# Maxima scores of latent and context attention taken for four head pairs in a row, with new order tables

## The chip, the cores and the metric

The kernel runs on one core of one Trainium2 chip. The metric is the device time of one execution in microseconds (us). TensorE is called PE, VectorE DVE, ScalarE ACT, GpSimd POOL and SyncE SP, as in the profile.

## What is computed

Two layers of a pre-norm decoder run over 32 sequences of 256 tokens with 256 features. Six steps follow each other for every sequence, and each adds its result to x:

```python
x = x + latent_attention(layernorm(x))            # 16 heads of 16, keys and values through a latent of 64
x = x + head_attention(layernorm(x), ctx)         # per token, 16 heads of 64 attend to each other; ctx 256 x 256
x = x + mixture_of_depths(layernorm(x))           # half of the tokens go through a 256-1024-256 network
x = x + sparse_attention(layernorm(x))            # of each score row only the 25 largest keep their value
x = x + context_attention(layernorm(x), ctx, len) # 16 heads of 16, keys from len on are masked
x = x + ternary_linear(layernorm(x))
```

## The kernel before

Everything is float32 but for a few bf16 helpers. The six steps are cut into four streams. Stream m is latent attention. Stream h is head attention and, at its end, mixture of depths (MoD). Stream t is sparse attention. Stream c is context attention and the ternary linear step. The streams work on different sequences at the same time: in one lap, m has the newest sequence, h the one before, t the next older and c the oldest. A lap is one sequence's worth of work on each stream. The steady part of the program holds 28 laps.

Every stream is a Python generator for each engine, and each `yield` in it ends a chunk. `woven` draws the chunks of the four streams in the order that a table gives. `ORDER["pe"]`, `ORDER["act"]`, `ORDER["dve"]` and `ORDER["pool"]` are strings of the letters m, h, t and c, one letter for each chunk. They cover four laps and are repeated seven times; `ORDER_FIRST` and `ORDER_LAST` are the laps before and after. An engine runs its instructions strictly in that order, so a chunk that waits for a semaphore holds up all chunks behind it. `FILL` says at which chunks, and how often, `fill` (L423) adds a matmul without use to PE's queue.

Streams m and c share the buffers `bufM` and the four PSUM banks `bankM`, and so follow one another. Their attention is `tensor_at` on PE. The 16 heads are 8 pairs; with 2 halves of the queries this makes 16 units. The keys of a pair (2 heads of 16 rows) lie in one strip of 32 partitions, and there are four such strips in each half `e` of `kT` and `q2`. First come the maxima: eight chunks of two units each, a pair in one of the strip couples (0, 1) and (2, 3), in `at_scores` (L494; the mask is added by the matmul of L489 in stream c). Each unit fills one bank, and DVE reduces it to the row maximum in `scores_max` (L504). Two chunks with their four units fill the four banks. Then POOL splits the maxima in three bf16 parts (L513), `shift_rows` (L528) and `shift_copy` bring them into rows, and `at_scores_T` (L550, L553) makes the scores transposed, two units to a chunk, in three banks. `exps_T` (L567) takes the exponential, and `at_values_T` (L580) multiplies with the values into `bankM[2]`. `at_out_pe1`, `at_out_dve` and `at_out_pe2` (L630, L639, L643, L652) divide by the sums.

Stream t scores a head pair in `at_scores` in its own banks `bankT`, ACT copies the scores to `sc` (L1019), and DVE finds the 25 largest of each row with four rounds of MAX8 (L1068) and MATCH_REPLACE8 (L1072) over two halves. POOL then makes the exponents from `wk` and `sc` (L1093, L1096, L1102, L1105), ACT takes the exponential (L1029), PE transposes (L595), ACT copies (L604), and PE multiplies with the values (L615). The heads are numbered r0 to r15 below. Stream t of a sequence begins only when MoD of the same sequence has added its update (L947), and when its own lap before has ended with the add of L688; then come layer norm (L427 to L461), projections (L467, L475) and the first scores. Selection of the next lap cannot begin before that.

MoD at the end of stream h is this on PE: the score row, then the chunk `sel` (L793, L797), which waits for ACT's pick matrix (L879), which waits for DVE's ranks (L930, L934); then the first layer in two chunks (L808), Gelu on ACT (L890), the second layer in eight (L814, L815) and the chunk `u` (L820).

## Time and profile before

| What | Value |
|---|---|
| median of three runs | 5935.59 us (5928.25 to 5955.03) |
| the profiled execution | 5922.4 us, of which the span is 5920.6 us |
| PE busy | 5310.9 us, 90% of the span |
| DVE busy | 4492.6 us, 76% |
| ACT busy | 3746.6 us, 63% |
| POOL busy | 2304.2 us, 39% |
| granted TensorE clock, mean | 0.95 of full speed |

Busy time counts a stretch once, however many instructions overlap in it. Matmuls in different strips of the array overlap, and so do consecutive ones with their tails; what a run of matmuls costs is read from the start of the run to the start of the next. A float32 matmul stands as two records. DVE's instructions overlap by their fixed part as well.

### The profile page before, as it was taken

To read this page: it belongs to the slowest core of one execution; us is meant where nothing else is said; L and a number is where in the kernel's file an instruction comes from. 1 tells how busy PE (TensorE), PEld (TensorE's weight loads), DVE (VectorE), ACT (ScalarE), POOL (GpSimd) and SP (SyncE) were. 2 spreads that over 40 slices of the span, in tenths; PEclk is the share of its full clock that TensorE was granted. 3 is DMA by queue.
4 is the path that set the end of the run, shared out by engine and by line. 5 is a ranking of instruction groups with operands and counts; after the bars stand their busy time and mean duration, and the time that the engine had idled before them with its cause. 6 is when DMAs were issued, how large, how long until landed. Compare 5 with 4: busy or idle time off the path is not lost.

```text
span 5920.6 us, 113246 instructions
## 1 busy us (share of the span) xinstructions
PE 5310.9 (90%) x39450; PEld 3769.4 (64%) x39450; DVE 4492.6 (76%) x16125; ACT 3746.6 (63%) x9377; POOL 2304.2 (39%) x4100
## 2 busy tenths in 40 slices
PE   7899989999989989989899989999989999989987
PEld 4666666666667666666666666666666666666654
DVE  2577787777787777887777787777787777788684
ACT  3566666666676666666666676666666666666642
POOL 0244443334443433443334443334443334443341
PEclk7899999999999999999999999999999999999876
DMA  2000000000000000000000000000000000000000
GB/s 90 6 5 7 7 8 8 5 8 7 7 8 8 5 8 5 9 8 8 5 8 7 7 9 8 5 8 7 7 8 8 5 8 7 7 8 8 1 4 6
DMA packets 29342, 52.98 MB, mean 9 GB/s; under 512 B 8145, under 2 KB 9810, under 8 KB 27986
## 3 DMA queue, kind: packets, MB, share of 16 engines
q1 hardware_dynamic: 28770, 45.73, 2.5%
q8 instruction: 313, 5.13, 0.4%
q14 instruction: 259, 2.12, 0.1%
HBM read 37.33 MB, written 8.39 MB: 8 GB/s over the span
## 4 chain that ended last, share of the span: by engine, by line
PE 42%; DVE 36%; ACT 14%; issue 4%; POOL 2%; ACTq 0%; DVEq 0%; POOLq 0%
DVE wk L1072 13%; DVE m L1068 9%; PE bankH L737 8%; PE bankM L494 4%; DVE m_nm L504 4%; DVE m_last L1068 3%; ACT xk_area L835 3%; PE bankM L467 3%; PE bankH L760 2%; ACT xq_area L835 2%; PE bankH L808 2%; PE bankH L814 2%; PE bankT L475 2%; PE bankT L467 2%; PE bankM L475 2%
## 5 line engine op out<-in xcount | busy, mean ns | idle before, releaser
L1072 DVE MATCH_REPLACE8 wk<-m,wk 128x256 f32<-128x256 f32 x2048 | 822.5, 409 | 0.0
L1093 POOL TENSOR_SCALAR mx<-m 128x2 f32<-128x2 f32 x512 | 114.3, 223 | 1737.7 <-DVE wk L1072 1732.4
L504 DVE TENSOR_REDUCE m_nm<-bankM 128x2 f32<-128x512 f32 x1024 | 651.8, 682 | 148.3 <-PE bankM L494 146.0
L1068 DVE MAX8 m<-wk 128x8 f32<-128x256 f32 x2048 | 759.9, 413 | 0.0
L1102 POOL TENSOR_TENSOR t_pr<-wk,sc 128x256 f32<-128x256 f32 x1024 | 739.2, 742 | 2.5 <-PE bankT L595 1.3
L1105 POOL TENSOR_TENSOR t_pr<-t_pr,sc 128x256 f32<-128x256 f32 x1024 | 729.4, 733 | 0.0
L835 ACT ACTIVATE xk_area<-bankH,xb 64x256 f32<-64x256 f32 x1024 | 479.7, 468 | 244.2 <-PE bankH L737 225.5
L1029 ACT ACTIVATE t_pr<-t_pr,t_nm 128x256 f32<-128x256 f32 x1024 | 476.5, 510 | 155.9 <-POOL t_pr L1105 143.1
L553 PE MATMUL bankM<-m_q,m_kT 32*128 32x512 f32 x2048 | 552.7, 619 | 0.0
L494 PE MATMUL bankM<-m_kT,m_q 32*128 32x256 f32 x4096 | 526.2, 393 | 10.1 <-DVE m_nm L504 8.9
L595 PE MATMUL bankT<-ident,t_pr 128*128 128x128 f32 x2048 | 339.2, 290 | 124.6 <-ACT t_pr L1029 122.1
L494 PEld LDWEIGHTS bankM<-m_kT,m_q 32*128 32x128 f32 x4096 | 376.3, 191 | 80.2 <-issue 23.4
L604 ACT ACTIVATE t_pt<-bankT 128x512 f32<-128x512 f32 x512 | 308.4, 602 | 175.5 <-PE bankT L595 171.1
L1072 DVE MATCH_REPLACE8 wk<-m_last,wk 128x256 f32<-128x256 f32 x1024 | 411.4, 409 | 0.0
L1072 DVE MATCH_REPLACE8 wk<-m,sc 128x256 f32<-128x256 f32 x1024 | 411.3, 409 | 0.0
L1068 DVE MAX8 m<-sc 128x8 f32<-128x256 f32 x1024 | 379.8, 413 | 29.5 <-ACT sc L1019 28.2
L595 PEld LDWEIGHTS bankT<-ident,t_pr 128*128 128x128 f32 x2048 | 236.7, 145 | 258.7 <-ACT t_pr L1029 209.0
L567 ACT ACTIVATE m_pT<-bankM,keymask 128x512 f32<-128x512 f32 x512 | 338.0, 692 | 96.4 <-PE bankM L553 93.5
L1019 ACT ACTIVATE sc<-bankT 128x512 f32<-128x512 f32 x512 | 306.4, 602 | 119.6 <-PE bankT L494 116.6
L1068 DVE MAX8 m_last<-wk 128x8 f32<-128x256 f32 x1024 | 379.7, 413 | 0.0
L580 PE MATMUL bankM<-m_pT,m_va 128*32 128x256 f32 x4096 | 355.4, 427 | 18.0 <-ACT m_ot L587 14.5
L567 ACT ACTIVATE m_pT<-bankM 128x512 f32<-128x512 f32 x512 | 282.6, 594 | 106.6 <-PE bankM L553 104.5
(224 smaller groups left out, 11691.4 us busy)
## 6 DMA issues: line engine op xcount, KB each, us to landing
xin<-x_in SPq DMA_DIRECT2D x32, 256.0 KB, 2.6
ctxA<-ctx_in SPq DMA_DIRECT2D x32, 256.0 KB, 2.6
ctxB<-ctx_in SPq DMA_DIRECT2D x32, 256.0 KB, 2.6
out<-x SPq DMA_DIRECT2D x32, 256.0 KB, 2.0
w<-w_w SPq DMA_DIRECT2D x2, 1024.0 KB
xwq<-w_xwq SPq DMA_DIRECT2D x1, 1024.0 KB
xwk<-w_xwk SPq DMA_DIRECT2D x1, 1024.0 KB
xwv<-w_xwv SPq DMA_DIRECT2D x1, 1024.0 KB
```

Source lines behind the costliest of these rows:

```text
L494: last = nc.tensor.matmul(bank[x][:, j * S:(j + 1) * S], b["q2"][r:r + 32, e, j, t * P:(t + 1) * P], b["kT"][r:r + 32, e, :], start=not ma ...
L504: nc.vector.tensor_reduce(b["nm"][:, i % 2, 2 * (i // 2) + x, :], banks[u % 4][:].rearrange("p (j s) -> p j s", j=2), AX.X, ALU.max, negat ...
L553: nc.tensor.matmul(bank[x][:], b["kT"][r:r + 32, e, c * P:(c + 1) * P], b["q2"][r:r + 32, e].rearrange("p j s -> p (j s)"), start=False, s ...
L567: nc.scalar.activation(b["pT"][c][:, x, :], bank[(0, 1, 3)[(2 * i + x) % 3]][:], ACT.Exp, bias=0.0 if bias is None else bias[:, c:c + 1]). ...
L595: last = nc.tensor.transpose(bank[:, (2 * c + j) * P:(2 * c + j + 1) * P], b["pr"][:, u % 2, j, c * P:(c + 1) * P], w["ident"][:])
L737: last = nc.tensor.matmul(bank[:, hp * S:(hp + 1) * S], w[wt][:, d, c:c + P], src[:, d, :], start=(d == 0), stop=(d == ND - 1))
L835: nc.scalar.activation(dst[0:XD, :, 8 * h:8 * h + 8].rearrange("p (j a) u -> p j a u", a=2), bankH[1 - TURNS.index("vqk"[which] + str(quad ...
L1029: nc.scalar.activation(b["pr"][:, u % 2, t, :], sp_[:, u % 2, t, :], ACT.Exp, bias=b["nm"][:, u, t:t + 1], scale=-1.0 / BIG).then_inc(g["s ...
L1068: link.inc(nc.vector.max(top, src[:, t, :]))
L1072: m = nc.vector.match_replace(out=wk[:, k, t, :], in_to_replace=take, in_values=src[:, t, :], imm_value=-BIG)
L1102: nc.gpsimd.tensor_tensor(taken[:, u % 2, t, :], wk[:, u % 2, t, :], sc[:, u % 3, t, :], ALU.subtract).then_inc(g["sp_tk"], 1)
L1105: nc.gpsimd.tensor_tensor(sp_[:, u % 2, t, :], taken[:, u % 2, t, :], sc[:, u % 3, t, :], ALU.mult).then_inc(g["sp_mul"], 1)
```

## The change

For the maxima, `pair_scores` takes four units at once, one in each strip and each with a bank of its own (`SIDE = 4`): eight chunks of an attention become four. A group waits until DVE has reduced all four units of the group before. Units are renumbered: four strips first, then the half of the queries, then `e`. The transposed scores keep two units to a chunk (`DEEP = 2`), but in the new numbering a chunk of strips 0 and 1 is followed by one of strips 2 and 3; the values take the heads and the PSUM halves accordingly. The order of operations of a unit, the waits on semaphores between engines and all instructions of ACT, DVE and POOL keep their kind and number. The order tables of all four engines are new, and so are the numbers of fills: 53 in four laps before, 91 after. In the new tables of PE the chunks of MoD from `sel` to `u` stand farther ahead in stream t. Before, `sel` stood behind the transpose of r14 and `u` at the end of the same lap of stream t. Now `sel` stands behind the transpose of r11, and `u` behind that of r13 in three laps of four and of r15 in one. On DVE, the ranks stand behind the end of r11 or within r12, where they stood behind r15.

The core of the diff (the strings of the order tables are left out):

```diff
...
+SIDE, DEEP = 4, 2
...
-FILL = {"t": ["00020100", "02010111", "00020101", "02010011"],
-        "h": ["20111000100", "00211000000", "00121000100", "01111100000"],
-        "c": ["00", "12", "21", "12"],
-        "m": ["110", "010", "110", "010"]}
...
+FILL = {"t": ["00002000", "00012121", "22021003", "02132010"],
+        "h": ["01213100000", "13010010000", "11103112130", "02012102022"],
+        "c": ["10", "00", "20", "03"],
+        "m": ["110", "023", "110", "233"]}
...
-CHUNKS = {"pe": dict(h=57, t=39, c=34, m=33),
+CHUNKS = {"pe": dict(h=57, t=39, c=30, m=29),
...
         def strip(pr):
             return pr // 4, 32 * (pr % 4)
 
-        def at_scores(n, b, bank, i, masked=False):
+        def at_scores(n, b, bank, i):
 
             m, t = i // 2, i % 2
-            for x in range(2):
-                if masked:
-                    r = strip(2 * m + x)[1]
-                    nc.tensor.matmul(bank[x][:], mask_lhs[r:r + 32, :], mrow[r:r + 32].rearrange("p t s -> p (t s)"), start=True, stop=False,
-                                     skip_group_check=True)
             for j in range(2):
                 for x in range(2):
                     e, r = strip(2 * m + x)
                     last = nc.tensor.matmul(bank[x][:, j * S:(j + 1) * S], b["q2"][r:r + 32, e, j, t * P:(t + 1) * P],
+                                            b["kT"][r:r + 32, e, :], start=True, stop=True)
+                    if j == 1:
+                        last.then_inc(g[n + "_s"], 1)
+
+        def pair_scores(n, b, units, masked):
+
+            if masked:
+                for u in units:
+                    r = 32 * (u % 4)
+                    nc.tensor.matmul(bankM[u % 4][:], mask_lhs[r:r + 32, :], mrow[r:r + 32].rearrange("p t s -> p (t s)"), start=True, stop=False,
+                                     skip_group_check=True)
+            for j in range(2):
+                for u in units:
+                    e, t, k = u // 8, u // 4 % 2, u % 4
+                    r = 32 * k
+                    last = nc.tensor.matmul(bankM[k][:, j * S:(j + 1) * S], b["q2"][r:r + 32, e, j, t * P:(t + 1) * P],
                                             b["kT"][r:r + 32, e, :], start=not masked, stop=True, skip_group_check=masked)
                     if j == 1:
                         last.then_inc(g[n + "_s"], 1)
 
-        def scores_max(dve, n, b, banks, u):
-
+        def scores_max(dve, n, b, u):
+
+            e, t, k = u // 8, u // 4 % 2, u % 4
             yield
             dve.wait_ge(*at(g[n + "_s"], u + 1))
-            i, x = u // 2, u % 2
-            nc.vector.tensor_reduce(b["nm"][:, i % 2, 2 * (i // 2) + x, :], banks[u % 4][:].rearrange("p (j s) -> p j s", j=2),
+            nc.vector.tensor_reduce(b["nm"][:, t, 4 * e + k, :], bankM[k][:].rearrange("p (j s) -> p j s", j=2),
                                     AX.X, ALU.max, negate=True).then_inc(g[n + "_nm"], 1)
 
         def shift_split(pool, n, b):
...
             act.wait_ge(*at(g[n + "_m3p"], 1))
             nc.scalar.activation(b["m3"][:], bank[:], ACT.Copy).then_inc(g[n + "_m3"], 1)
 
-        def at_scores_T(pe, n, b, bank, i):
-
-            m, c = i // 2, i % 2
-            bank = [bank[(0, 1, 3)[(2 * i + x) % 3]] for x in range(2)]
-            yield
-            if i == 0:
+        def pair_scores_T(pe, n, b, units):
+
+            bank = lambda v: bankM[(0, 1, 3)[v % 3]]
+            if units[0] == 0:
                 pe.wait_ge(*at(g[n + "_m3"], 1))
-            elif i >= 2:
-                pe.wait_ge(*at(g[n + "_ex"], 2 * i - 1))
-            else:
-                pe.wait_ge(*at(g[n + "_ex"], 1))
-            for x in range(2):
-                r = strip(2 * m + x)[1]
-                nc.tensor.matmul(bank[x][:], sel_b[r:r + 32, 2 * m + x, :], b["m3"][r:r + 32, :], start=True, stop=False, skip_group_check=True)
-            for x in range(2):
-                e, r = strip(2 * m + x)
-                nc.tensor.matmul(bank[x][:], b["kT"][r:r + 32, e, c * P:(c + 1) * P],
+            if units[-1] >= 3:
+                pe.wait_ge(*at(g[n + "_ex"], units[-1] - 2))
+            for v in units:
+                e, k = v // 8, v % 4
+                r = 32 * k
+                nc.tensor.matmul(bank(v)[:], sel_b[r:r + 32, 4 * e + k, :], b["m3"][r:r + 32, :], start=True, stop=False, skip_group_check=True)
+            for v in units:
+                e, c, k = v // 8, v // 4 % 2, v % 4
+                r = 32 * k
+                nc.tensor.matmul(bank(v)[:], b["kT"][r:r + 32, e, c * P:(c + 1) * P],
                                  b["q2"][r:r + 32, e].rearrange("p j s -> p (j s)"), start=False, stop=True,
                                  skip_group_check=True).then_inc(g[n + "_st"], 1)
 
-        def exps_T(act, n, b, bank, i, bias=None):
-
-            c = i % 2
+        def exps_T(act, n, b, i, bias=None):
+
+            c = i // 2 % 2
             for x in range(2):
                 yield
                 act.wait_ge(*at(g[n + "_st"], 2 * i + x + 1))
...
                     act.wait_ge(*at(g[n + "_pv"], i - 1))
                 if i == 0 and bias is not None:
                     act.wait_ge(*at(g["mask_row"], 2))
-                nc.scalar.activation(b["pT"][c][:, x, :], bank[(0, 1, 3)[(2 * i + x) % 3]][:], ACT.Exp,
+                nc.scalar.activation(b["pT"][i % 2][:, x, :], bankM[(0, 1, 3)[(2 * i + x) % 3]][:], ACT.Exp,
                                      bias=0.0 if bias is None else bias[:, c:c + 1]).then_inc(g[n + "_ex"], 1)
 
         def at_values_T(pe, n, b, bank, i):
 
-            m, c = i // 2, i % 2
+            e, c, y = i // 4, i // 2 % 2, i % 2
             yield
             pe.wait_ge(*at(g[n + "_ex"], 2 * i + 2))
             if i == 4:
                 pe.wait_ge(*at(g[n + "_ot"], 1))
+            if i % 4 == 0:
+                fill("c" if n == "crs" else "m", i // 4 + (n == "mla"), bank[:, S:S + P])
             for x in range(2):
                 for j in range(2):
                     r = 32 * (2 * x + j)
-                    last = nc.tensor.matmul(bank[r:r + 32, S * (m % 2):S * (m % 2 + 1)], b["va"][:, c, 4 * m + 2 * x + j, :],
-                                            b["pT"][c][:, x, S * j:S * (j + 1)], start=(c == 0), stop=(c == 1))
+                    last = nc.tensor.matmul(bank[r:r + 32, S * y:S * (y + 1)], b["va"][:, c, 8 * e + 4 * y + 2 * x + j, :],
+                                            b["pT"][i % 2][:, x, S * j:S * (j + 1)], start=(i % 4 == 0), stop=(c == 1), skip_group_check=True)
             last.then_inc(g[n + "_pv"], 1)
 
         def at_copy_ot(act, n, b, bank, half):
...
 
         def tensor_at(pe, n, masked):
             b = bufM
-            for i in range(8):
-                yield
-                if i == 0:
+            for u in range(0, 2 * PAIRS, SIDE):
+                yield
+                if u == 0:
                     pe.wait_ge(*at(g[n + "_kT"], 1))
                     pe.wait_ge(*at(g[n + "_qT"], 2))
                     pe.wait_ge(*at(g[n + "_va"], 1))
                     if masked:
                         pe.wait_ge(*at(g["mask_row"], 1))
-                elif i == 1 and masked:
-                    past(pe, "mla_x")
-                elif i == 1 and here("c"):
-                    pe.wait_ge(*at(g["lin_o"], 1))
-                elif i >= 2:
-                    pe.wait_ge(*at(g[n + "_nm"], 2 * i - 2))
-                at_scores(n, b, [bankM[2 * i % 4], bankM[(2 * i + 1) % 4]], i, masked)
+                if u <= 2 < u + SIDE:
+                    if masked:
+                        past(pe, "mla_x")
+                    elif here("c"):
+                        pe.wait_ge(*at(g["lin_o"], 1))
+                if u >= 4:
+                    pe.wait_ge(*at(g[n + "_nm"], u - 4 + SIDE))
+                pair_scores(n, b, range(u, u + SIDE), masked)
             yield from shift_rows(pe, n, b, bankM[2])
-            for i in range(9):
-                if i < 8:
-                    yield from at_scores_T(pe, n, b, bankM, i)
-                if i >= 1:
-                    yield from at_values_T(pe, n, b, bankM[2], i - 1)
-                if i in (2, 6):
-                    fill("c" if masked else "m", i // 4 + (not masked), bankM[2][:, S:S + P])
+            done = 0
+            for v in range(0, 2 * PAIRS, DEEP):
+                yield
+                pair_scores_T(pe, n, b, range(v, min(v + DEEP, 2 * PAIRS)))
+                while 2 * done + 2 <= v:
+                    yield from at_values_T(pe, n, b, bankM[2], done)
+                    done += 1
+            while done < PAIRS:
+                yield from at_values_T(pe, n, b, bankM[2], done)
+                done += 1
             yield from at_out_pe1(pe, n, b, [bankM[3], bankM[2]], 2)
             yield from at_out_pe2(pe, n, b, bankM[2])
 
...
             b = bufM
             yield from shift_copy(act, n, b, bankM[2])
             for i in range(8):
-                yield from exps_T(act, n, b, bankM, i, bias)
+                yield from exps_T(act, n, b, i, bias)
                 if i == 5:
                     yield from at_copy_ot(act, n, b, bankM[2], 0)
             yield from at_copy_ot(act, n, b, bankM[2], 1)
...
 
         def vector_at(dve, n):
             for u in range(2 * PAIRS):
-                yield from scores_max(dve, n, bufM, bankM, u)
+                yield from scores_max(dve, n, bufM, u)
             yield from at_out_dve(dve, n, bufM, [bankM[3], bankM[2]])
...
```

## Rows read from the trace of the kernel before

**Rows 1.** The page: busy time by engine, and the chain that ended last.
```profile
PE 5310.9 (90%) x39450; PEld 3769.4 (64%) x39450; DVE 4492.6 (76%) x16125; ACT 3746.6 (63%) x9377; POOL 2304.2 (39%) x4100
...
PE 42%; DVE 36%; ACT 14%; issue 4%; POOL 2%; ACTq 0%; DVEq 0%; POOLq 0%
```

**Rows 2.** Busy time by stretch: start:end, length, then engines, clock, DMA.
```profile
1946.00:1991.30 45.30, 40.68 (x251) 33.92 (x251) 16.34 (x46) 20.58 (x49) 9.05 (x13) 0.96 0.00 1
1991.30:2120.50 129.20, 118.06 (x974) 79.80 (x972) 122.59 (x458) 95.89 (x248) 64.35 (x117) 1.00 0.03 10
2120.50:2167.60 47.10, 42.67 (x274) 35.26 (x274) 17.79 (x48) 22.71 (x51) 7.88 (x12) 0.96 0.00 1
2167.60:2300.70 133.10, 120.41 (x962) 81.44 (x958) 122.49 (x457) 94.36 (x243) 62.95 (x115) 0.97 0.03 9
...
1946.00:2655.90 709.90, 645.50 (x4922) 462.11 (x4922) 559.98 (x2013) 467.48 (x1173) 288.53 (x512) 0.98 0.02 7
```

**Rows 3.** Timeline, all engines: from the end of one selection to the next.
```profile
1945.56 0.40 DVE L1072 MATCH_REPLACE8 wk<-m_last,wk 128x256 f32<-128x256 f32 x1
...
1948.52 0.69 ACT L876 ACTIVATE xv<-iota,rank 128x128 f32<-128x128 f32 x2 [2.17 <-DVE xv L934]
...
1949.85 1.87 PE L793 MATMUL bankH<-xv,lnH_xn 128*128 128x128 f32 x8 [4.14 <-ACT xv L879]
...
1955.17 0.60 PE L595 MATMUL bankT<-ident,t_pr 128*128 128x128 f32 x4
...
1970.49 1.89 PE L467 MATMUL bankM<-ctxB,cwk 128*128 128x256 f32 x8
1972.22 1.89 PE L475 MATMUL bankM<-cwv,ctxB 128*128 128x256 f32 x8
...
1991.34 0.75 DVE L1068 MAX8 m<-sc 128x8 f32<-128x256 f32 x2
```

**Rows 4.** Groups by line in 1946.0 to 2655.9, four laps, with releasers.
```profile
L504 DVE TENSOR_REDUCE m_nm<-bankM 128x2 f32<-128x512 f32 x128 | 81.4, 683 | 12.2 <-PE bankM L494 11.9
...
L907 DVE TENSOR_REDUCE xnm<-bankH 128x4 f32<-128x512 f32 x32 | 21.9, 684 | 22.1 <-PE bankH L760 22.1
...
L793 PE MATMUL bankH<-xv,lnH_xn 128*128 128x128 f32 x32 | 8.1, 433 | 18.3 <-ACT xv L879 18.3
```

**Rows 5.** Timeline of PE: chunks of two strips as they are now.
```profile
1987.50 0.39 PE L489 MATMUL bankM<-mrow,mask_lhs 32*128 32x512 bf16 x2 [0.23 <-issue]
...
1988.57 0.39 PE L489 MATMUL bankM<-mrow,mask_lhs 32*128 32x512 bf16 x2
...
2076.82 2.00 PE L494 MATMUL bankM<-m_kT,m_q 32*128 32x256 f32 x16
2078.74 0.66 PE L750 MATMUL bankH<-ident,lnH_xT 128*128 128x128 f32 x4
```

**Rows 6.** Timeline of PE: two streams' chunks in four different strips.
```profile
2085.89 0.48 PE L494 MATMUL bankM<-m_kT,m_q 32*128 32x256 f32 x2
2085.91 0.48 PE L494 MATMUL bankT<-t_kT,t_q 32*128 32x256 f32 x2
...
2086.86 0.60 PE L494 MATMUL bankM<-m_kT,m_q 32*128 32x256 f32 x4
```

**Rows 7.** Timeline of PE: two fills between their neighbours.
```profile
2034.66 0.71 PE L423 MATMUL bankT<-xwq 128*128 128x128 f32 x4
2035.31 0.39 PE L550 MATMUL bankM<-m_m,sel_b 32*128 32x512 bf16 x2
```

**Rows 8.** Timeline of the last lap of stream t, with little beside it.
```profile
5825.17 0.41 DVE L1072 MATCH_REPLACE8 wk<-m_last,wk 128x256 f32<-128x256 f32 x1
...
5829.07 0.66 PE L595 MATMUL bankT<-ident,t_pr 128*128 128x128 f32 x4
...
5837.19 0.69 DVE L688 TENSOR_TENSOR x<-bankT,x3b 128x512 f32<-128x512 f32 x1 [3.53 <-PE bankT L475]
```

**Rows 9.** Busy time by stretch: the granted clock after PE's wait.
```profile
1950.10:1953.50 3.40, 3.40 (x20) 2.26 (x20) 0.00 (x0) 1.45 (x4) 0.86 (x1) 0.50 0.02 5
```

112 lines of the change are left out of this document (54 added, 58 removed).

## The prediction

> **What bounds the kernel now.** I first read the busy shares of the page. PE is busy for 90% of the span and DVE for 76%, but the chain that ended last gives PE 42% and DVE 36% [rows 1]. So the two take turns, and the next view has to say where. The busy times by stretch show it. One lap has two parts, which repeat with little change in all 28 steady laps. In the first, between the end of one selection and the start of the next, PE is busy for 40.7 us of 45.3 and 42.7 of 47.1, while DVE has only 16 to 18 us of work. I call it the gap; the two shown have a mean of 46.2 us. In the second, the selection of sixteen heads, DVE is busy for 122.6 us of 129.2 and 122.5 of 133.1. Four laps take 709.9 us, so a lap takes 177.5 us, 46.2 of gap and 131.3 of selection [rows 2]. PE is no idle bystander there: it is busy for 118.1 and 120.4 us [rows 2].
>
> The timeline shows what the gap is made of. Selection ends at 1945.96 (1945.56 and 0.40). DVE then ranks the tokens for MoD and ACT's pick matrix starts at 1948.52; PE stands at `sel` until 1949.85, idle for 4.14 us. The transpose of r15, the last head, starts at 1955.17, behind `sel` and the first half of the first layer. Then PE works nearly without a break until the first scores of stream t are out, and the first MAX8 of the next selection starts at 1991.34 [rows 3]. In the selection, DVE's waits in four laps are 22.1 us for the scores of stream h and 11.9 us for the maxima scores [rows 4].
>
> **The maxima groups.** Two chunks of two strips in stream m take 1.92 us, 0.96 each; a masked one takes 1.07 us from start to start [rows 5]. The new group of four strips is seen once already, where a chunk of stream m meets one of stream t in other strips: sixteen records take 0.97 us, from 2085.89 to 2086.86, as long as eight do now [rows 6]. I take 0.97 for a group in stream m and add 0.21 for the four masks, which is what a pair of them costs now (1.07 less four slots of 0.216, an eighth of the 1.73 us of a projection [rows 3]). In a lap, stream m goes from 8 x 0.96 = 7.7 to 4 x 0.97 = 3.9, and stream c from 8 x 1.07 = 8.6 to 4 x 1.18 = 4.7: together 7.7 us of PE less. The old tables let a chunk meet one in other strips now and then; for that I take off 1.6, which leaves 6.1. The bounds are 7.7 (nothing was shared) and 4.
>
> The Trainium skill (TensorE: Matmul & The Clock Gate, Measured speedup vs the span model) gives 3.07 times for four row strips. Sixteen records of 0.216 by that speedup would take 1.13 us rather than 0.97; an estimate by that page is 1.3 us less gain in a lap, inside the bounds. The row is this kernel's own operation, so I stay with it.
>
> **The fills.** Four laps have 38 fills more, 9.5 in a lap. Two take 0.65 us between their neighbours [rows 7], so this is 3.1 us of PE. They stand where the tables expect PE to wait, so they are hidden as long as PE does wait there; I count them all in PE's work. They also say something: the order expects more idle PE than before.
>
> **The transposed scores.** They keep their instructions, waits and banks. Chunks of other strips now follow each other, but a wait for ACT or a chunk of values stands between them; I take nothing, with bounds of 0 and -1 us.
>
> **The new order: the gap.** In the gap, the new tables change most. `sel` to `u` are no longer in it, but for one `u` in four laps. So the transpose of r15 no longer waits for the ranks, the pick matrix, `sel` and the first layer. How soon it can start is seen in the last lap, where little runs beside it: selection ends at 5825.58 and the transpose starts at 5829.07, 3.5 us later [rows 8]. Now it is 9.2 us (1945.96 to 1955.17) [rows 3]. That takes away 5.7 us.
>
> From that transpose to the first MAX8 it is 36.2 us now [rows 3]. I listed PE's chunks there from both tables and priced them with start-to-start times. A projection of eight records is 1.73 us (1970.49 to 1972.22) [rows 3]. Before there are 11 such blocks in each lap; after there are 13, 14, 14 and 12, a mean of 13.25, since stream h is farther ahead: +3.9 us. The rest of MoD leaves, 6.9 us (the second half of the first layer at 2.1, the second layer at 3.9, `u` at 0.95, one of four kept): -6.7. Some maxima chunks, small transposes and one output step change places: +0.1. The sum is -2.7, so 33.5 us. PE does this work without a break only if its order also suits the chain of stream t. That chain alone, from the end of selection to the add, takes 12.3 us (5825.58 to 5837.88) [rows 8], far less than PE's work in the gap, but the new order has some 5 us of other chunks between the output projection and the next layer norm, where a statistic on DVE, a power on POOL and a normalisation must pass. I add 1.5 us for PE's waits, with bounds of 0 and 5. The gap becomes 3.5 + 33.5 + 1.5 = 38.5 us, 7.7 less.
>
> **The new order: the selection.** What left the gap must be done here. On DVE it is the ranks, 2.6 us (1945.96 to 1948.52) [rows 3]; the other small steps that change sides give -0.3. So DVE's work goes from 122.5 to 124.8. Its idle time is now 131.3 - 122.5 = 8.8 us. Its largest part, 22.1 / 4 = 5.5 us for the scores of stream h [rows 4], may shrink, since h starts the selection farther ahead. New waits may come: the ranks for the score row, and the maxima, whose groups take all four banks. I let these cancel and add 0.4. The selection becomes 134.0 us, the lap 172.5, 5.0 less than now.
>
> PE must agree. It is busy for 645.5 / 4 = 161.4 us in a lap [rows 2]. After: 161.4 - 6.1 + 3.1 = 158.4. With 37 in the gap, 121.4 of 134.0 us are left in the selection, 90.6%; today it is 238.5 of 262.3, 90.9% [rows 2]. So PE fits, but has no room to make the selection shorter by much.
>
> **The sum.** 28 laps x -5.0 = -140 us. The laps at both ends have their own tables, partly without one of the streams; there I take nothing, with bounds of 25 us either way. The profiled execution took 5922.4 us, 13 less than the median of the runs. Its sum is 5782; against the median of 5935.6 it is 5795 us, 2.4% less.
>
> **The rivals.**
>
> *Hand-over of four banks (slower).* Now PE fills two banks while DVE reduces the other two. After the change, a group needs all four maxima of the group before. If DVE comes to each batch before PE is done, it waits for a group and a semaphore, about 1.2 us, eight times a lap: 9.6 us. The waits on maxima of today, 11.9 / 4 = 3.0 us [rows 4], are in this, so 6.6 are new. The lap takes 179.1 us and the kernel 5981, slower by 0.8%. It decides from 5 us a lap. Against it: in DVE's new table two rounds of selection stand between most batches, 2.9 us, enough for a group if PE's queue is not late. For it: PE is busy for over 90% of this part, and is late now and then already. With a slip on top it would be 6040.
>
> *The clock (no change).* After PE's wait of 4.14 us, a stretch of 3.4 us was granted only half the clock, 0.50, at 1950.10 [rows 9], and this inside the gap, where PE sets the pace. Over four laps the granted clock is 0.98 [rows 2]. The Trainium skill (TensorE: Matmul & The Clock Gate, HAM oscillation — how this bites in real kernels) has idle PE lose its clock, which speaks against a change that gives PE less to do; the trace agrees. If the mean fell to 0.95 it would cost 3% of a lap, 5.3 us, and nothing would be left: 5943 us. Against it: the wait at `sel` leaves the gap, and there are more fills.
>
> *PE lets go of the selection (much faster).* If the 5.5 us for stream h go and PE's waits in the gap stay near 0, the lap takes 172.5 - 5.5 - 1.5 = 165.5, and the kernel 5600. PE would have to be busy for 95.7% of it, more than in any part but the gap.
>
> *Four strips don't run side by side (the change doesn't do what it says).* Then PE keeps its 7.7 us: 166.1 us of work at a share of 0.909 is a lap of 182.7, and 6080 us. Rows 6 speak against it.
>
> **Chances and range.** The forecast (a lap of 169.5 to 175.5, 5710 to 5880 us) gets 0.60; much faster 0.12; no change by clock or by half of the hand-over 0.12; the full hand-over 0.13; no four strips 0.03. The range goes from 5660, in the middle of the fast case, to 5975, which takes in no change and half of the slow case. About 0.5% is what a measurement of this kernel can tell from no change, so: faster by more 0.72, within it 0.12, slower by more 0.16.
>
> **What would show it.** In the profile after, the maxima matmuls of streams m and c should stand in groups of sixteen records, 0.97 us apart, with some 6 us of PE less in a lap. The gap should be near 38.5 us with no wait at `sel` in it, and the transpose of r15 some 4 us after the end of selection. DVE should be busy for about 125 us of a selection of 134. The prediction is wrong if DVE's waits for maxima scores grow past 5 us in a lap, if PE idles by more than 5 us in the gap behind stream t's steps, if the granted clock falls under 0.96 in the steady laps, or if the wait at `sel` now holds up the transposes on which DVE's selection hangs.

## The result and the profile after

The changed kernel takes 5976.6 us (median of 10 runs, 5941.3 to 6036.2), where the kernel before takes 5935.3 us in the same sessions. The ratio is 1.0078, with a 95% interval of 1.0054 to 1.0101; it leaves out two executions of the kernel before, of 11369 and 15016 us, and one of the changed kernel, of 6036 us, as slow ones. So it is slower by 0.8%; the prediction was 5795, with a range up to 5975. The profiled execution took 6010.1 us, with a span of 6008.3.

The page of the changed kernel, to be read against [rows 1]: busy time by engine, and the chain that ended last.

```profile
PE 5436.8 (90%) x39974; PEld 3769.5 (63%) x39974; DVE 4540.9 (76%) x16125; ACT 3737.0 (62%) x9377; POOL 2282.5 (38%) x4100
...
PE 58%; DVE 22%; ACT 11%; issue 4%; POOL 4%; DVEq 0%; ACTq 0%; POOLq 0%
```

PE's busy time rose by 126 us, though the change takes work from it, and its share of the chain rose from 42% to 58%. Busy time by stretch says where (columns as in [rows 2]; the granted clock of PE is the third number from the end). First a gap and a selection of four laps in turn, then all four laps, then two stretches of 47.8 us and two single laps:

```profile
2518.00:2560.70 42.70, 39.26 (x258) 29.99 (x258) 14.47 (x40) 22.54 (x47) 8.23 (x13) 1.00 0.03 8
2560.70:2690.50 129.80, 121.34 (x1046) 82.85 (x1045) 126.80 (x463) 98.69 (x257) 63.12 (x116) 1.00 0.03 7
2690.50:2731.50 41.00, 38.79 (x237) 32.49 (x236) 16.02 (x43) 25.35 (x53) 8.18 (x13) 0.96 0.03 7
2731.40:2880.20 148.80, 138.32 (x1002) 87.91 (x1001) 126.50 (x463) 91.30 (x241) 63.49 (x115) 0.84 0.02 7
2880.20:2921.60 41.40, 40.76 (x257) 33.58 (x256) 15.74 (x43) 27.05 (x58) 8.17 (x13) 1.00 0.03 7
2921.50:3063.20 141.70, 128.76 (x1023) 86.42 (x1022) 127.66 (x467) 90.44 (x238) 63.22 (x115) 0.90 0.03 7
3104.70:3243.30 138.60, 123.52 (x958) 81.31 (x957) 123.18 (x456) 87.23 (x232) 62.79 (x116) 0.89 0.02 7
2518.00:3243.30 725.30, 671.78 (x5037) 468.02 (x5037) 566.78 (x2012) 469.25 (x1179) 285.31 (x513) 0.92 0.03 7
2751.50:2799.30 47.80, 47.73 (x236) 24.18 (x234) 28.88 (x115) 25.29 (x71) 15.98 (x28) 0.50 0.00 1
2558.90:2606.70 47.80, 45.35 (x375) 29.27 (x378) 45.15 (x165) 42.46 (x101) 18.66 (x37) 1.00 0.02 7
2690.50:2880.20 189.70, 177.01 (x1237) 120.32 (x1236) 142.41 (x505) 116.65 (x294) 71.67 (x128) 0.87 0.02 7
3412.00:3585.80 173.80, 160.63 (x1237) 112.71 (x1236) 142.16 (x505) 116.30 (x294) 71.81 (x129) 0.95 0.02 7
```

The gaps did shrink: 42.7, 41.0, 41.4 and 41.4 us, where [rows 2] have 45.3 and 47.1. The selections did the rest. The one with a clock of 1.00 took 129.8 us, and with its gap the lap took 172.5 us, as forecast for the mean. The other three had clocks of 0.84, 0.90 and 0.89 and took 148.8, 141.7 and 138.6 us. The order tables cover four laps, which differ in themselves, so one lap is no proof; the shortest of each of the four kinds in this trace took 168.7, 173.4, 182.0 and 176.8 us (from one gap's start to the next), a mean of 175.2. The last two rows are the plainest: they are the same lap of the table, with the same 1237 matmuls, four laps apart. At a clock of 0.95 it took 173.8 us, at 0.87 189.7. All seven passes of this lap are alike in that: with 13.7 and 17.1 us at half clock (a granted clock of 0.50) they took 173.4 and 173.8 us, with 44.4 (twice) 185.5 and 185.6, with 51.2 (three times) 188.9 to 189.8. So 1 us of half clock cost this lap some 0.43 us. By this estimate the 17.5 us more of a mean lap (26.3 for 8.8, in the table below) cost some 7.5 us, where the lap misses its forecast of 172.5 by 7.4.

The rows of 47.8 us show what half the clock is. From 2751.5 PE was busy for 47.73 of 47.80 us at 0.50 and has 236 matmul records, where a stretch of equal length at full clock has 375; DVE got 28.9 us of work done rather than 45.2. Before, no such stretch in the steady laps was longer than 6.8 us (one of 3.4 is in [rows 9]); after, they go up to 51.2 us. In a mean of 24 steady laps, half clock in the selection went from 3.7 to 26.0 us. PE's busy time there went from 119.5 to 127.4 us, 7.9 more, and the selection grew by 8.1 us, with PE's share nearly the same (91.2% and 91.5%).

Where such a stretch begins is seen in the timeline of PE (start, duration; in brackets the idle time before and its releaser). First a group of four strips with its masks and stream t's scores behind it, then the last group of that attention, and the start and the end of the 47.8 us:

```profile
2727.63 0.40 PE L496 MATMUL bankM<-mrow,mask_lhs 32*128 32x512 bf16 x4
2727.86 1.03 PE L502 MATMUL bankM<-m_kT,m_q 32*128 32x256 f32 x16
2728.72 1.03 PE L486 MATMUL bankT<-t_kT,t_q 32*128 32x256 f32 x8
...
2744.34 1.03 PE L502 MATMUL bankM<-m_kT,m_q 32*128 32x256 f32 x16
...
2747.22 0.60 PE L603 MATMUL bankT<-ident,t_pr 128*128 128x128 f32 x4
2750.79 0.41 PE L536 MATMUL bankM<-ident_b,m_sp 128*32 128x128 bf16 x16 [2.96 <-POOL m_sp L527]
2751.13 1.72 PE L768 MATMUL bankH<-xk_area,xq_area 72*128 72x128 f32 x8
2752.78 0.61 PE L555 MATMUL bankM<-m_m,sel_b 32*128 32x512 bf16 x2
2753.18 1.92 PE L559 MATMUL bankM<-m_q,m_kT 32*128 32x512 f32 x4
...
2795.92 1.65 PE L420 MATMUL bankH<-xwq 128*128 128x128 f32 x6
```

The sixteen records of L502 take 0.86 us (2727.86 to 2728.72), and 1.09 with their masks (from 2727.63), so the four strips do run side by side. The masks say that this group belongs to stream c. Three more of the same attention follow, the last at 2744.34. At 2750.79 PE has waited 2.96 us in `shift_rows` (L536) for POOL's split of the maxima. Then the four records of L559 take 1.92 us where they take about 1.0 at full clock. The full clock is back after a stretch with six records of fills (L420). In 27 of the steady laps of this trace there are 39 half-clock stretches. Of the 19 that last over 20 us, 18 begin inside of such a wait of 2.2 to 3.0 us at L536 or within 2 us of its end, and none of these waits is without a half-clock stretch. After that very wait of 2.96 us the stretch lasted 47.8, 44.4, 17.1, 13.7 or 51.2 us in different laps. All these waits are in stream c's attention, in three laps of four; in the fourth lap stream c waits 0.63 us, and stream m never waits longer than 0.73 us. Before, PE never waited at this place. Groups by line in 2518.0 to 3243.3, to be read against [rows 4]:

```profile
L512 DVE TENSOR_REDUCE m_nm<-bankM 128x2 f32<-128x512 f32 x128 | 80.7, 679 | 31.2 <-PE bankM L502 31.2
...
L915 DVE TENSOR_REDUCE xnm<-bankH 128x4 f32<-128x512 f32 x32 | 21.9, 685 | 35.1 <-PE bankH L768 35.1
...
L801 PE MATMUL bankH<-xv,lnH_xn 128*128 128x128 f32 x32 | 4.4, 281 | 1.1 <-ACT xv L887 1.1
...
L536 PE MATMUL bankM<-ident_b,m_sp 128*32 128x128 bf16 x128 | 3.7, 243 | 9.9 <-POOL m_sp L527 9.9
```

In the same groups of the kernel before, that last line has an idle time of 0.0:

```profile
L528 PE MATMUL bankM<-ident_b,m_sp 128*32 128x128 bf16 x128 | 3.3, 221 | 0.0
```

The maxima's waits on DVE rose from 11.9 to 31.2 us, but most of that is not in the selections. There, DVE's waits are these: first the clean selection from 2560.7, then the one from 2731.4.

```profile
DVE m L1076 <- ACT sc L1027: 2.0, 3, 0.9
DVE xnm L915 <- PE bankH L768: 1.7, 2, 1.3
...
DVE xnm L915 <- PE bankH L768: 14.8, 4, 8.0
DVE m L1076 <- ACT sc L1027: 4.3, 1, 4.3
...
DVE m_nm L512 <- PE bankM L502: 0.7, 2, 0.5
```

So at full clock DVE waits 3.7 us in a selection; at half clock in 47.8 us of it, it waits 14.8 us for the scores of stream h alone and 0.7 for maxima.

### The profile page after: what moved, and what is told of

Same layout as the page of the kernel before. It is cut to its first block, busy times and chain, and to the rows that moved or that the text cites. A ratio compares the mean times of both kernels' runs of the same rounds, so it can differ in the third digit from the quotient of the medians.

```text
span 6008.3 us, 114323 instructions
## 1 busy us (share of the span) xinstructions
PE 5436.8 (90%) x39974; PEld 3769.5 (63%) x39974; DVE 4540.9 (76%) x16125; ACT 3737.0 (62%) x9377; POOL 2282.5 (38%) x4100
## 4 chain that ended last, share of the span: by engine, by line
PE 58%; DVE 22%; ACT 11%; issue 4%; POOL 4%; DVEq 0%; ACTq 0%; POOLq 0%
PE bankH L745 7%; PE bankM L559 6%; DVE wk L1080 6%; DVE m_nm L512 5%; PE bankM L588 4%; DVE m L1076 4%; PE bankH L768 4%; PE bankH L785 3%; PE bankT L603 3%; PE bankT L486 3%; PE bankM L502 2%; PE bankM L555 2%; PE bankT L472 2%; PE bankT L464 2%; PE bankT L623 2%
## 5 line engine op out<-in xcount | busy, mean ns | idle before, releaser
L559 PE MATMUL bankM<-m_q,m_kT 32*128 32x512 f32 x2048 | 662.6, 731 | 0.0
L603 PE MATMUL bankT<-ident,t_pr 128*128 128x128 f32 x2048 | 363.7, 305 | 78.9 <-ACT t_pr L1037 77.9
L603 PEld LDWEIGHTS bankT<-ident,t_pr 128*128 128x128 f32 x2048 | 250.5, 153 | 256.1 <-ACT t_pr L1037 172.2
L588 PE MATMUL bankM<-m_pT,m_va 128*32 128x256 f32 x4096 | 377.1, 450 | 29.3 <-ACT m_ot L595 16.0
L915 DVE TENSOR_REDUCE xnm<-bankH 128x4 f32<-128x512 f32 x256 | 175.2, 685 | 293.3 <-PE bankH L768 292.6
L768 PEld LDWEIGHTS bankH<-xk_area,xq_area 72*128 72x128 f32 x2048 | 305.4, 229 | 137.1 <-issue 67.9
L970 POOL TENSOR_TENSOR xp<-xp,xrr 128x512 f32<-128x512 f32 x192 | 199.7, 1040 | 469.5 <-DVE xrr L921 468.7
```

The lines of the kernel that those rows point to most:

```text
L559: nc.tensor.matmul(bank(v)[:], b["kT"][r:r + 32, e, c * P:(c + 1) * P], b["q2"][r:r + 32, e].rearrange("p j s -> p (j s)"), start=False, s ...
L588: last = nc.tensor.matmul(bank[r:r + 32, S * y:S * (y + 1)], b["va"][:, c, 8 * e + 4 * y + 2 * x + j, :], b["pT"][i % 2][:, x, S * j:S * ( ...
L603: last = nc.tensor.transpose(bank[:, (2 * c + j) * P:(2 * c + j + 1) * P], b["pr"][:, u % 2, j, c * P:(c + 1) * P], w["ident"][:])
L768: last = nc.tensor.matmul(bankH[0][:, i * P:(i + 1) * P], xqT[:, c, :], xkT[:, c, :], start=True, stop=True)
```

## The experiments

The theory is this. POOL's split comes later than PE now wants it, PE idles for 2 to 3 us, its clock falls to half, and the small matmuls behind it (few rows, few columns) do not bring it back for tens of us. The rivals are the hand-over of four banks, the new units, the ends, and a PE path that is too long by itself. This is what the runs of all kernels gave. Lap, gap and selection are means over 24 steady laps of the profiled execution. Half clock is the time of a lap at 0.50. "PE at full clock" is PE's busy time in a lap less half of its time at half clock. This is an estimate: it takes the same work as twice as long at half clock (1.92 us for 1.02 at L559), and PE as busy all through it. In before and in e6 PE idles for part of it (1.6 of 8.8 us and 3.4 of 18.6), so there the column is too low by 0.8 and 1.7 us.

| kernel | us, median | ratio to before [95%] | lap | gap | selection | half clock | PE at full clock |
|---|---|---|---|---|---|---|---|
| before | 5935.3 | 1 | 177.6 | 46.5 | 131.1 | 8.8 | 157.1 |
| after | 5976.6 | 1.0078 [1.0054, 1.0101] | 179.9 | 40.7 | 139.2 | 26.3 | 153.4 |
| e1_shift_fill4 | 5987.1 | 1.0092 [1.0075, 1.0109] | 179.2 | 40.7 | 138.5 | 20.8 | 155.5 |
| e2_no_fills | 6036.8 | 1.0176 [1.0161, 1.0191] | 181.5 | 40.6 | 140.8 | 36.4 | 146.5 |
| e3_two_strips | 5992.2 | 1.0101 [1.0086, 1.0116] | 180.2 | 41.0 | 139.2 | 26.0 | 154.1 |
| e5_old_order_new_units | 5944.0 | 1.0018 [1.0006, 1.0031] | 178.4 | 46.4 | 131.9 | 11.5 | 156.1 |
| e6_old_order_four_strips | 6091.1 | 1.0268 [1.0247, 1.0289] | 183.4 | 47.8 | 135.6 | 18.6 | 150.8 |
| e7_fill_in_wait8 | 5894.0 | 0.9937 [0.9915, 0.9959] | 177.5 | 40.8 | 136.7 | 14.6 | 157.8 |
| e8_fill_in_wait16 | 6058.0 | 1.0205 [1.0171, 1.0238] | 181.6 | 40.7 | 140.9 | 16.9 | 161.3 |
| e9_old_ends | 5986.5 | 1.0087 [1.0052, 1.0122] | 178.4 | 40.5 | 137.9 | 22.9 | 153.5 |
| e10_fill_in_wait_c8 | 5938.3 | 1.0000 [0.9986, 1.0013] | 178.0 | 41.0 | 137.0 | 18.9 | 155.8 |
| e11_fills_behind_wait | 5950.1 | 1.0029 [1.0020, 1.0039] | 177.9 | 41.2 | 136.7 | 16.1 | 156.3 |
| e12_before_fill8 | 5992.5 | 1.0100 [1.0080, 1.0121] | 180.6 | 47.0 | 133.6 | 12.2 | 159.2 |
| e13_c8_and_later | 5937.0 | 1.0013 [0.9993, 1.0033] | 178.3 | 41.0 | 137.3 | 14.6 | 157.9 |
| e14_wait8_and_fills | 5907.6 | 0.9955 [0.9937, 0.9973] | 176.9 | 40.7 | 136.2 | 7.8 | 160.8 |
| e15_wait8_m_only | 5961.3 | 1.0054 [1.0023, 1.0085] | 178.9 | 40.8 | 138.1 | 21.2 | 155.5 |

One profiled execution stands for a kernel in the last five columns, and it need not be near the median: e7's took 5923.0 us, the longest of its eight, and after's 6010.1. A difference of medians is clear of noise only where the intervals of the ratios lie apart.

**Matmuls behind the wait.**

```diff
 def shift_rows(pe, n, b, bank):
     yield
     pe.wait_ge(*at(g[n + "_sp"], 4))
+    more(4, bank[:, 0:P])    # four matmuls 128x128 without use
```

> The changed kernel with one addition: in both attentions, four matmuls without use (as the fills are) stand behind the wait for POOL's split of the maxima, ahead of the matmuls of shift_rows; 8 more in a lap. Theory A (the clock): in the changed kernel PE waits 2.2 to 3.0 us there, the granted clock falls to half, and the matmuls of the transposed scores and values that follow don't bring it back for 20 to 48 us. Four full-height matmuls right behind the wait should bring it back at once: the time at half clock in the steady laps (693 us in the changed kernel, 232 before) goes to 350 or less, and the kernel takes 5850 to 5920 us. Theory B (the waits between PE and DVE over the four banks cost the time, the clock is a by-product): the matmuls are only more work for PE, 8 x 0.3 = 2.4 us a lap, and the kernel takes 5980 to 6045 us.

5987.1 us, no gain, and in the range of the rival B. In the kind of lap with the wait of 2.96 us the stretch is now 13.7 or 17.1 us, but in the two other kinds with a long wait it is 23.9 to 30.7 us each time, and a lap still has 20.8 us of half clock. The wait itself stays:

```profile
2737.81 1.34 PE L426 MATMUL bankM<-xwq 128*128 128x128 f32 x8 [2.97 <-POOL m_sp L533]
```

Theory A had four full-height matmuls behind the wait bring the clock back at once; they neither prevent the fall nor do that.

**No fills at all.** The steady `FILL` table is set to zeros, 22.75 matmuls fewer in a lap.

> The changed kernel without the 91 fills of four steady laps (22.8 in a lap, some 0.3 us of PE each, 6.8 us). Theory A (the clock): the fills hold the clock up; without them the granted clock of the steady laps falls further below 0.92 and the kernel is slower than 5976 us, 6020 to 6150. Theory B and the step of my prediction that counts fills as PE's work: PE gets up to 6.8 us a lap back, 5790 to 5900 us.

6036.8 us: 60 us slower with 6.9 us less of PE's work in a lap (0.30 for each fill). The half clock grows from 26.3 to 36.4 us. The clock outweighs the work here. Four laps:

```profile
2518.00:3246.40 728.40, 663.05 (x4806) 450.92 (x4805) 565.53 (x2013) 463.25 (x1167) 284.76 (x513) 0.89 0.02 7
```

**Two strips after all.** Only the order of matmuls inside the chunk changes.

```diff
-                pair_scores(n, b, range(u, u + SIDE), masked)
+                pair_scores(n, b, range(u, u + 2), masked)
+                pair_scores(n, b, range(u + 2, u + SIDE), masked)
```

> The changed kernel with its tables and waits, but in each group of four units the matmuls of strips 0 and 1 come first, all of them, and those of strips 2 and 3 behind: two strips side by side as before, in the same chunk. By my prediction's step (four strips save 6.1 us of PE in a lap, and PE is short) it should be slower than the changed kernel by up to 170 us, near 6100 us. Theory A (the clock): PE has more to do while DVE and POOL work on the maxima, so its wait for the split is shorter and the clock falls less; the two effects nearly cancel, 5940 to 6010 us. Theory B (four banks handed over at once): the last strips come later, so DVE's waits for maxima grow beyond 31 us in four laps: 6050 or more.

5992.2 us. The intervals of the ratios of e3 and after overlap, so the 16 us between them are not clear of noise, and they are far from a step of 170. The timeline says why:

```profile
2726.72 0.39 PE L496 MATMUL bankM<-mrow,mask_lhs 32*128 32x512 bf16 x2
2726.95 0.38 PE L502 MATMUL bankM<-m_kT,m_q 32*128 32x256 f32 x2
2726.97 0.39 PE L496 MATMUL bankM<-mrow,mask_lhs 32*128 32x512 bf16 x2
2727.16 1.05 PE L502 MATMUL bankM<-m_kT,m_q 32*128 32x256 f32 x14
2728.15 1.99 PE L745 MATMUL bankH<-ctxA,xwk 128*128 128x256 f32 x8
...
PE bankM L536 <- POOL m_sp L527: 9.5, 6, 3.0
```

Two couples of different strips that stand right behind each other overlap in the main anyway. The group takes 1.43 us with its masks (2726.72 to 2728.15), where after's takes 1.09 and two masked chunks in the same strips took 2 x 1.07 [rows 5]. So what saves PE's time is for the most part that chunks in different strips follow each other with nothing between; the order within the group gives only 0.7 us a lap. The last line is PE's waits in four laps in `shift_rows` (total, number, longest): they stay, and so does the half clock.

**The old tables with the new units.** The order tables and fills of before, and `SIDE, DEEP = 2, 2`, so that only the numbering of the units and the transposed scores are new.

> The new numbering of units alone: the order tables, fills and two-strip chunks of the kernel before, with the units and the transposed scores in the new order of strips. Theory A (what cost the time in e6 are the groups of four, with the waits and the clock they bring): no change, 5915 to 5955 us. Rival (the new numbering itself makes PE slower or faster, since transposed scores in other strips follow each other and the values use both halves of a bank in turn): 5960 or more, or 5905 or less.

5944.0 us, a ratio of 1.0018. The new units cost at most 0.3%.

**The old tables with groups of four.** In the old tables the first of every two maxima chunks of m and c is dropped, and a group of four stands at the second's place.

> The four-strip groups alone, in the steady laps: the order tables and fills of the kernel before, where of each two neighbouring maxima chunks of PE one is left out and the group of four stands at the place of the later one; the laps at both ends keep two strips. The gap between two selections should stay at 46 us, since the mixture of depths stays in it. By the forecast's terms PE has 6 us less in the selection, where DVE's idle time is 8.8 us: 1 to 3 us a lap, 5850 to 5905 us. Theory A (the clock): the maxima's chunks are over sooner, PE waits longer for the split of the maxima, and the clock falls behind it: 5940 to 6010 us. Theory B: the hand-over of four banks, in tables made for two, shows as more than 31 us of DVE waits for maxima in four laps: 6000 or more.

6091.1 us, the slowest of all. PE's work is 6.3 us a lap less than before, and 5.5 with PE's idle time at half clock taken out of the estimate; this bears out the term of 6.1. But DVE now waits in one selection, from 2602.6 to 2736.4, as the first two lines say; the third is PE's waits in `shift_rows` in four laps:

```profile
DVE m_nm L534 <- PE bankM L524: 6.8, 4, 2.2
DVE xnm L937 <- PE bankH L790: 3.9, 4, 1.3
...
PE bankM L558 <- POOL m_sp L549: 2.8, 4, 1.1
```

Over four selections the maxima's waits are 24.8 us, where before has 9.4 and after 2.5. The hand-over of four banks is a real mechanism, though the half clock rose as well, from 8.8 to 18.6 us a lap, and this run does not part the two. The new tables, with two rounds of selection between the batches, avoid the hand-over. It is not why after is slow. The run says one thing more: with groups of four in the old tables, no wait in `shift_rows` is longer than 1.1 us. So the waits of 2.2 to 3.0 us come with the new tables and not with the groups alone.

**Matmuls ahead of the wait.** In both attentions PE gets eight matmuls without use ahead of `shift_rows`; e8 has sixteen. In stream c they lie where PE would idle. In stream m it would hardly idle, so there they are plain fills.

```diff
 def shift_rows(pe, n, b, bank):
     yield
+    pe.wait_ge(*at(g[n + "_nm"], 13))
+    more(8, bankM[0][:, 0:P])
     pe.wait_ge(*at(g[n + "_sp"], 4))
```

> The changed kernel, where PE works in the wait for the split of the maxima instead of after it: once the first of the last four maxima is read, eight matmuls without use go to the bank that it frees, and only then PE waits for the split. They lie in a wait of 2.2 to 3.0 us in three laps of four, so they cost the path next to nothing there. Theory A (the clock falls because of this wait, and what follows can't bring it back): the falls of 20 to 48 us behind it go, the half-clock time of a lap (26.3 us) goes to 14 or less, the selection shortens by half of what goes, and the kernel takes 5800 to 5900 us. Theory B (waits between PE and DVE cost the time): 16 matmuls more in a lap, no gain, 5970 to 6050 us.

5894.0 us. By the last column the kernel does 4.4 us more work in a lap and is 83 us faster than after, and 0.6% faster than before (0.9937 [0.9915, 0.9959]). It is the best version found. The timeline at the place of the 2.96 us:

```profile
2695.90 1.95 PE L426 MATMUL bankM<-xwq 128*128 128x128 f32 x16
2699.03 0.41 PE L544 MATMUL bankM<-ident_b,m_sp 128*32 128x128 bf16 x16 [1.18 <-POOL m_sp L533]
2699.37 1.16 PE L776 MATMUL bankH<-xk_area,xq_area 72*128 72x128 f32 x8
2700.46 0.39 PE L563 MATMUL bankM<-m_m,sel_b 32*128 32x512 bf16 x2
2700.68 1.02 PE L567 MATMUL bankM<-m_q,m_kT 32*128 32x512 f32 x4
```

The wait is cut to 1.18 us and L567 takes 1.02 us. The cure is not complete: at 2703, in this same lap, a stretch of 44.4 us begins nevertheless, after no more than this wait of 1.18 us and one of 1.15. In four of the six laps of this kind there is no such stretch.

> As e7, with sixteen matmuls instead of eight: some 4.5 us of PE each time, 1.5 to 2 us longer than the wait. Theory A: the clock is held at least as well as in e7, but the path gets 3 us a lap: 5850 to 5960 us, slower than e7 by up to 85 us, and still no slower than the changed kernel. Theory B: 6050 us or more.

6058.0 us, a miss for the theory that I held: there is little more half clock than in e7 (16.9 us), but the selection grows by 4.2 us. Eight take 1.95 us, so sixteen take 3.9 and outlast the wait of 2.96; after them PE waits for no split any more. In e7 what was left of stream c's waits is 1.18, 0.24, 1.22 and 0 us in the four laps, 0.7 in the mean, so of 1.95 us more some 1.3 are new; in stream m all 1.95 are. That is an estimate of 3.2 of the 4.2 us. The half clock, longer by some 2 us, may be the rest; no run shows it.

> As e7, but the eight matmuls in the wait only in stream c; in stream m PE has seven us of other work between the last maxima and the split and hardly waits, so there they were plain work (8 x 0.3 = 2.4 us a lap). Theory A: the clock is held as in e7 and PE has 2.4 us a lap less to do: 5830 to 5890 us, faster than e7 by up to 60. Rival (the matmuls of stream m held the clock too): 5900 to 5960 us.

> The changed kernel with the eight useless matmuls in stream m's attention alone. Of the 82 us that both places brought, stream c's alone brought 38. Theory A (each place has its own wait and its own half-clock stretch behind it): m alone brings the rest, 30 to 60 us, so the median is 5915 to 5950 us. Rival B (one place does nothing without the other, since a stretch that starts anywhere is only ended by chance): no more than 15 us, 5960 us or more.

With the eight in stream c alone it takes 5938.3 us, in stream m alone 5961.3. So they bring 38 and 15 us, and together 83. PE's waits in `shift_rows` in four laps, first in e10, then in e15:

```profile
PE bankM L545 <- POOL m_sp L533: 3.7, 5, 1.2
...
PE bankM L545 <- POOL m_sp L533: 8.8, 4, 3.0
```

After has 9.9 there. So e15 leaves the long waits as they were, since all of them are stream c's, and its 15 us are not clear of noise (1.0023 to 1.0085, where after has 1.0054 to 1.0101). The theory that each place has its own wait was wrong, and the rivals of both runs had the time right. e10 is the clean trial of the wait: with this wait alone cut, 1.0000 for 1.0078, and 18.9 us of half clock for 26.3. The further 44 us from e10 to e7 are clear of noise too, and come from eight matmuls a lap that fill no wait. They take the half clock from 18.9 to 14.6 us, as fills do. Whether 83 is really more than 38 and 15 together these runs can't tell: the difference of 30 us is about their uncertainty.

**More fills, without touching the wait.**

```diff
-        "c": ["10", "00", "20", "03"],
+        "c": ["66"] * 4,
```

> The changed kernel with more fills where its tables have them in stream c, in the transposed scores behind the wait: 6 and 6 in every lap, where there are 6 in all in four laps. They can't keep the clock from falling in the wait; theory A says that full-height matmuls bring it back sooner: no half-clock stretch behind the wait longer than about 17 us, where 20 to 48 us stand now. The 10.5 fills more a lap cost 3.1 us of PE; the shorter stretches give back about that: 5930 to 6000 us. Rival (they are only more work, and the clock stays down whatever is in the queue): 6040 to 6080 us.

5950.1 us: 10.5 more full-size matmuls a lap make the kernel 26 us faster. No stretch is longer than 17.1 us, though every wait for the split is still there. Together with e10 this shows that both the wait and what stands behind it count: the one starts the half clock, and full-size matmuls behind it shorten it. That it is the small matmuls which keep it is argued from what runs in the long stretches; no run changed them.

> e10 and, on top, the fills of stream c at 3 and 6 in every lap, some 7.5 a lap more: in e7 some laps still have a stretch of 17 to 48 us at half clock that begins behind the wait. Theory A: if these go, 3.7 us a lap of PE time come back for 2.2 us of fills: within 30 us of e10. Rival (e10 leaves little to gain, PE is short): slower than e10 by 50 to 70 us.

5937.0 us, no gain over e10's 5938.3, as theory A allowed. Its profiled execution has the half clock and PE's work of e7's (14.6, and 157.9 for 157.8), yet the median is 43 us higher. So these two columns alone don't fix the time; it matters too where the fills stand.

**The control: eight matmuls in the kernel before,** where PE has no wait at that place (stream c alone, as in e10).

> Control: the kernel before, with the same eight matmuls at the same place of stream c. There PE doesn't wait for the split. If e7 is faster only because of the wait in which its matmuls lie, then here they are 2.4 us a lap of plain work in a selection where PE is busy for 90%: 5960 to 6010 us. Rival (such matmuls help the clock wherever they stand): 5900 us or less.

5992.5 us, slower by 1.0%. Here the matmuls are plain work: they are no gift of their own. In the changed kernel, which has more half clock to lose, eight a lap without a wait did pay (e7 against e10).

**The ends.** After's steady laps, with the tables, fills and two-strip chunks of before in the first and last laps.

> The changed kernel in the 28 steady laps, but with the tables, fills and two-strip chunks of the kernel before in the laps at both ends. By the traces, the changed kernel loses 2.3 us in each steady lap and some 24 us at the ends (I had taken 0, with bounds of 25 either way). If the ends do cost that by themselves, this takes 24 us less than the changed kernel, 5940 to 5960 us. Rival: the ends are slower only because the steady laps hand them another state; then it is no faster, 5965 to 5990 us.

5986.5 us, no faster: the forecast of 5940 to 5960 lies below its interval, which starts at 5965. So the tables of the ends are not what costs the time. The prediction's 0 for the ends was still not exact. The profiled executions of before and after differ by 88 us, of which 28 laps x 2.3 us are 64; the other 24 lie outside the steady laps, within the stated bounds of 25, and this run does not say why.

**Both cures.** The matmuls of e7 and the fills of e11.

> The changed kernel with eight useless matmuls ahead of the wait for the negated maxima in both attentions (as in the version that took 5894 us) and twelve fills a lap behind them in stream c (as in the one that took 5950 us). Theory A (the half clock is started by PE's wait for the split and kept alive by the small matmuls behind it, so that both fills act): half clock falls under 10 us a lap, the laps come to 173 to 176 us, the median to 5840 to 5900 us. Rival B (once the clock holds, every further fill only lengthens PE's path, which carries the selection too): half clock falls likewise, but the lap stays at 177 to 180 us and the median is 5900 to 5970 us.

5907.6 us, between the two. This run separates the clock from the work. The half clock falls to 7.8 us a lap, less than before has; no stretch is longer than 10.2 us; the clock is 0.98 again. Yet the lap takes 176.9 us. Selections of two laps, and all four laps:

```profile
2522.80:2656.70 133.90, 127.45 (x1100) 88.99 (x1099) 126.64 (x463) 98.48 (x257) 63.16 (x116) 1.00 0.03 7
...
2876.80:3017.40 140.60, 127.92 (x1075) 89.28 (x1074) 126.66 (x467) 90.44 (x238) 62.75 (x115) 0.96 0.02 7
...
2483.80:3192.40 708.60, 660.09 (x5211) 475.73 (x5211) 565.63 (x2012) 465.20 (x1172) 284.83 (x512) 0.98 0.03 7
```

The selection with clock 1.00 takes 133.9 us, where after's clean one of the same lap takes 129.8. PE has 6.1 us more work in it (127.5 for 121.3). In the one at 0.96, DVE waits for stream h's scores:

```profile
DVE xnm L923 <- PE bankH L776: 8.0, 3, 4.2
```

So the rival of that run had it right: the clock is back, and the work that brought it back has taken PE's time instead. The empty work of 7.4 us a lap is twice what the change saves of PE, and of the 5 us a lap that were forecast 0.7 are left. The time is in the rival's range (5900 to 5970); the lap fell 0.1 us short of its 177.

## Why the prediction was wrong

**What was right.** PE's saving: PE's work at full clock went from 157.1 to 153.4 us, 3.7 less, where 3.0 were forecast; e6 measured the groups alone at 5.5 to 6.3 (forecast 6.1), and e2 the fills at 0.30 each (forecast 0.33). The shortest group takes 0.97 us to what follows it, and 1.09 with masks (forecast 0.97 and 1.18); the medians over 24 laps are 1.08 and 1.19. The r15 transpose: in the gap from 2518.0 it starts 3.5 us after the selection ends, at 2521.54, as read from [rows 8]. `sel` costs PE 1.1 us in four laps, not 18.3. PE idles for 1.6 us in a gap, the mean of four in a row (3.4, 2.2, 0.6, 0.3); I had put 1.5. DVE's work in the selection is 126.0 us (mean of four), for 124.8.

**What was a little off.** The gap is 40.7, not 38.5: PE has 40.0 us of work in it (39.3, 38.8, 40.8, 41.1), where I listed chunks for 37. That is 2.2 us a lap, some 60 us for the kernel.

**The step that failed** is the selection, and in it the line "so PE fits": 121.4 us of PE in 134.0. The selection takes 139.2 us, and PE is busy for 127.4 of them, 26.0 at half clock. In the one selection of the table at a clock of 1.00 it held: 121.3 us of PE in 129.8, and a lap of 172.5. I had taken PE's work as a number of microseconds. It is one only at a given clock. With 17.5 us more of a lap at half clock, up to 8.7 us are added to PE's work, more than twice the 3.7 saved. PE's share of the selection stayed at 91.2 to 91.5%, and the selection grew with PE's busy time, by 8.1 us for 7.9.

The mechanism stood among the rivals, but at the wrong place and size. I looked at the one wait that [rows 9] showed with a half-clock stretch behind it, saw that it would leave the gap, and counted this against the rival. I did not ask whether the shorter PE queue would come early somewhere else. It does so at `shift_rows`. In both kernels the split waits for the last of the sixteen maxima of the attention. In the lap shown, 6.4 us pass from the start of PE's last group (2744.34) to `shift_rows` (2750.79), and the new table gives PE less than that to do. Since e6 has no such wait over 1.1 us with the same groups, and e3 keeps it with two strips, it is the order that makes it. Neither did I ask what stands behind the wait. In the gap it was followed mostly by full-height matmuls (`sel`, the first layer), and the stretches ended after 3.4 or 6.8 us; in the selection it is followed by matmuls of 32 or 72 rows and small transposes, and lasts up to 51.2 us. My price for the rival, a mean clock of 0.95 for 5.3 us, was too low: it was 0.92 in the four laps shown, and 5977 us rather than 5943. In the rival of no four strips a sum is off as well: it takes back 7.7 us of a saving that was counted as 6.1, so it should be 164.5 us of PE rather than 166.1, a lap of 181.0 and about 6030 us. No conclusion hangs on it.

Of the signs that were named, the clock under 0.96 is the one that came. The one for the maxima, over 5 us a lap, came by its letter (31.2 / 4 = 7.8), but was badly put: only 2.5 us in four laps lie in the selections, where they count. The wait for the hand-over cost nothing in after; in e6, with the old tables, it would have decided.

That idle time costs PE its clock is seen in the 18 stretches above and, the other way round, in e10. The Trainium skill (TensorE: Matmul & The Clock Gate, HAM oscillation — how this bites in real kernels) says the same of a PE that waits between bursts, though the waits there are longer than the 2.2 to 3.0 us here. The Trainium skill (the same page, Part 1: The HAM clock gate) has a busy PE get the full clock back soon. The rows do not agree with that for the small matmuls and transposes that ran here: PE was busy for 47.73 of 47.80 us and stayed at half clock, so here the measurement decides.

**What stays open.** Why the same wait in the same lap is followed now by 13.7 and now by 51.2 us of half clock; which of the matmuls behind the wait keep it; what the 24 us outside the steady laps are; and whether a table that gives PE useful work during the split would reach 172.5 us throughout. The last wasn't tried. The shortest laps of after, with a mean of 175.2 us, speak for 175 or less, and e14 shows that empty work is not the way: its laps take 176.9 us.

## What to carry to other kernels

Here PE's clock fell where it idled, so taking 3.7 us of work from it lengthened its busy time by 5.0 us a lap: before pricing a saving on PE, look for the wait in which the engine will now arrive too early, and for the kind of matmuls that stand behind it. In these traces the wait of 4.1 to 4.7 us at `sel`, ahead of full-size matmuls, was followed by 3.4 or 6.8 us of half clock; waits of 2.2 to 3.0 us ahead of small ones by 13.7 to 51.2 us. Where such a wait can't be filled with useful work, empty work that fits in it is worth a trial: eight matmuls in stream c's waits brought 38 us. Too much of it costs: eight in each attention brought 83 us, and sixteen in each cost 81. To compare kernels, use PE's busy time less half of its half-clock time, and know that it is an estimate.

## What was unexpected in the hardware

- PE stayed at 1.2 GHz, half its clock, for 47.8 us while its records show it busy for 47.73 of them. What it ran there were matmuls in one to four strips of 32 rows, with 72 rows, and transposes.
- A wait of 2.2 to 3.0 us stood ahead of 18 of the 19 stretches over 20 us; the wait of 0.63 us at the same line in the selection from 2560.7 was not followed by any half clock. But in e7 a stretch of 44.4 us came after waits of only 1.18 and 1.15 us.
- Two couples of matmuls in different strips, issued one after the other, overlap nearly as well as four issued in turn: 1.43 us with masks for 1.09, where two chunks in the same strips took 2.14.
- The time of after's runs goes with the clock: spans of 5939.5, 5965.1, 5979.1, 6008.3 and 6015.6 us at mean clocks of 0.919, 0.914, 0.911, 0.906 and 0.905.
